# A hybrid three-kind layer stack on one core: the weighted sums of the feed-forward layers run as one block of 24 matmuls instead of three of 8

## The reference, cut to what matters

```python
gating = jax.nn.softmax(x @ W_gate.T, axis=-1)
indicator = jax.nn.one_hot(jnp.argmax(gating, axis=-1), H)
q, k, v = jnp.split(x @ W_qkv.T, 3, axis=-1)
k_shared = jnp.einsum('bth,bthd->btd', indicator, k)
v_shared = jnp.einsum('bth,bthd->btd', gating_top1, v)
att = jnp.einsum('bhqd,bkd->bhqk', q, k_shared) / sqrt(hd)   # 16 heads, hd = 16
att = softmax(where(causal, att, -inf))
y = jnp.einsum('bhqk,bkd->bhqd', att, v_shared)              # the weighted sums
...
x = x + attn_a(layernorm(x)); x = x + ffn(layernorm(x))
x = x + attn_b(layernorm(x)); x = x + ffn(layernorm(x))
```

## Time and profile before

| | before |
|---|---|
| median of 3 runs | 960.64 us (959.54 to 963.05) |
| profiled execution, its own time | 962.72 us |
| span of that execution in the trace | 961.0 us |
| mean granted TensorE clock | 0.972 of full |
| share of the span busy: PE, PEld, DVE, ACT, POOL | 93%, 73%, 74%, 56%, 45% |
| weighted sums of the feed-forward layers, matmul rows | L1748 512, L1751 256 |

### The profile page before, as it was taken

One profiled execution on the slowest core, in us unless ns is written; L12 is line 12 of the kernel. 1 busy time (PEld: TensorE's weight loads), 2 busy tenths in 40 slices (PEclk: granted clock), 3 DMA queues, 4 the chain that ended last, 5 costly groups with the idle time before them and its releaser, 6 DMA issues.

```text
span 961.0 us, 20310 instructions
## 1 busy us (share of the span) xinstructions
PE 891.1 (93%) x6766; PEld 700.0 (73%) x6766; DVE 709.6 (74%) x2331; ACT 534.0 (56%) x1410; POOL 436.4 (45%) x682
## 2 busy tenths in 40 slices
PE   6789989889999999978999999999999997999996
PEld 5677767767767776657878888788878776777763
DVE  6768888888778887664767767685858667888873
ACT  6536554553345455526667676757575762555555
POOL 2458879887756566342202112020202013556655
PEclk9769999999999999989999999999999999999999
DMA  6433333322112555002202020202011021232321
GB/s 197 63 54 56 55 45 55 54 49 43 35 35 58 128 119 139 2 13 45 45 1 45 1 45 2 44 2 45 16 30 41 5 33 32 39 63 47 73 48 35
DMA packets 51287, 46.63 MB, mean 49 GB/s; under 512 B 6624, under 2 KB 48624, under 8 KB 51184
## 3 DMA queue, kind: packets, MB, share of 16 engines
q1 hardware_dynamic: 51184, 45.34, 23.5%
HBM read 11.40 MB, written 2.10 MB: 14 GB/s over the span
## 4 chain that ended last, share of the span: by engine, by line
PE 38%; DVE 10%; issue 4%; ACT 1%; POOL 0%; DMA 0%; POOLq 0%; SPq 0%; ACTq 0%; DVEq 0%
PE bank L285 10%; PE bank L1937 5%; PE bank L1887 5%; PE bank L1945 4%; PE bank L1875 4%; DVE weights L1451 3%; PE bank L1710 3%; PE bank L1722 2%; DVE q_lo L1431 2%; DVE weights L1441 2%; PE bank L1707 2%; PE bank L1748 1%; ACT oT L962 1%; PE bank L1751 1%; DVE arena L1288 1%
## 5 line engine op out<-in xcount | busy, mean ns | idle before, releaser
L1288 DVE TENSOR_REDUCE arena<-bank 128x2 f32<-128x512 f32 (+1 forms) x192 | 130.5, 683 | 43.7 <-PE bank L1710 42.6
L904 ACT ACTIVATE weights<-bank 128x512 f32<-128x512 f32 x144 | 85.7, 596 | 112.9 <-PE bank L1722 111.8
L983 ACT ACTIVATE weights<-weights,neg_max 128x128 f32<-128x128 f32 (+1 forms) x256 | 113.8, 449 | 19.3 <-DVE neg_max L1441 19.3
L1441 DVE CUSTOM_DVE_ANT_0 weights<-bank,arena 128x128 f32<-128x128 f32 (+1 forms) x256 | 80.7, 352 | 56.6 <-PE bank L1937 54.8
L712 POOL TENSOR_SCALAR_AFFINE_SELECT weights<-weights 128x256 f32<-128x256 f32 x144 | 68.2, 475 | 105.0 <-ACT weights L904 104.9
L990 ACT ACTIVATE weights<-bank 128x384 f32<-128x384 f32 x128 | 62.8, 490 | 85.7 <-PE bank L1945 83.5
L1710 PE MATMUL bank<-kf_stack,q_stack 96*128 96x128 f32 (+1 forms) x512 | 109.6, 317 | 0.0
L1937 PE MATMUL bank<-kbT,arena 128*128 128x128 f32 (+1 forms) x512 | 105.1, 328 | 1.1 <-DVE y L420 0.9
L648 POOL TENSOR_SCALAR weights<-weights 128x512 f32<-128x512 f32 x64 | 97.9, 1539 | 12.5 <-ACT weights L807 12.3
L1451 DVE TENSOR_SCALAR weights<-weights,inv_sum 128x128 f32<-128x128 f32 (+1 forms) x256 | 84.3, 371 | 4.5
L285 PE MATMUL bank<-x_hi,wb_hi 128*128 128x256 f32 x256 | 83.5, 326 | 2.8 <-DVE q_lo L1431 2.8
(11 more groups left out here) (232 smaller groups left out, 2443.0 us busy)
## 6 DMA issues: line engine op xcount, KB each, us to landing
q_stack<-q_hi SPq DMA_DIRECT2D x96, 128.0 KB, 3.8
arena<-arena SPq DMA_DIRECT2D x64, 128.0 KB, 2.5
q_stack<-q_lo SPq DMA_DIRECT2D x48, 128.0 KB, 4.0
ka_stack<-k_hi SPq DMA_DIRECT2D x32, 76.5 KB, 3.8
x_all<-x SPq DMA_DIRECT2D x8, 256.0 KB, 5.1
st_wo<-b_wo SPq DMA_DIRECT2D x8, 256.0 KB, 3.1
arena<-b_wqn SPq DMA_DIRECT2D x8, 256.0 KB, 3.2
out<-x_all SPq DMA_DIRECT2D x8, 256.0 KB, 2.1
```

Source lines behind the costliest of these rows:

```text
L904: a.activation(s["pT"][(STEPS * b + k) % N_PT], p2[k % 2][:, :], ACT.Exp).then_inc(s["exp"], 1)
L983: last = a.activation(p, p, ACT.Exp, scale=-1.0, bias=neg_max[:, h % 4, t:t + 1], accum_out=sums[:, h % 4, t:t + 1])
L1288: v.tensor_reduce(into, p1[k % 2][:, :].rearrange("p (h k) -> p h k", h=n), AX.X, ALU.max, negate=True).then_inc(s["maxed"], 1)
L1441: last = v.tensor_tensor_reduce(out=probs[:, h % 4, part], in0=ps_s[h % 2][:, part], in1=mask_b[:, (1 - t) * P:2 * P], scale=1.0, scalar=F ...
```

## The change

`attend_f` loses its argument for the part and runs all three parts back to back. It stands where part 2 stood: octet 1 in step 3, octet 0 in step 9. The matmuls, their operands and the order in which a bank is written are the same; the two waits for the mask become one (all six items instead of four first).

```diff
-                def attend_f(b, o, part):
+                def attend_f(b, o):
...
-                    if part == 0:
-                        pe.wait_ge(*(at(sa, "oT", B - 1, 2) if s is sf[0] and (b, o) == (0, 0) else at(s, "oT", b, o)))
-                        if o == 0:
-                            pe.wait_ge(*at(s, "v_sel", b, 2))
-                    pe.wait_ge(*at(s, "causal", b, 6 * o + (6 if part == 2 else 4)))
+                    pe.wait_ge(*(at(sa, "oT", B - 1, 2) if s is sf[0] and (b, o) == (0, 0) else at(s, "oT", b, o)))
+                    if o == 0:
+                        pe.wait_ge(*at(s, "v_sel", b, 2))
+                    pe.wait_ge(*at(s, "causal", b, 6 * o + 6))
+                    for part in range(2):
+                        for j in range(G):
+                            half = slice(part * T, (part + 1) * T)
+                            mm(ps_o[j * VC:(j + 1) * VC, half], v_sh[b % 3][:, 0, :], items[j][:, half], start=part == 0,
+                               stop=False, skip_group_check=True)
                     for j in range(G):
...
+                        last = mm(ps_o[j * VC:(j + 1) * VC, :].rearrange("p (g q) -> p g q", g=2)[:, :, P:T],
+                                  v_sh[b % 3][:, 1, :],
+                                  items[4 + j // 2].rearrange("p (j g q) -> p j g q", j=2, g=2)[:, j % 2],
+                                  start=False, stop=True, skip_group_check=True)
+                    last.then_inc(s["o_ps"], 1)
...
-                    if k in (1, 3) and there(b - 2):
-                        attend_f(b - 2, 1, (k + 1) // 2)
-                    if k in (5, 7, 9, 11) and there(b - 1):
-                        attend_f(b - 1, k // 11, (k - 5) // 2 % 3)
+                    if k == 3 and there(b - 2):
+                        attend_f(b - 2, 1)
+                    if k == 9 and there(b - 1):
+                        attend_f(b - 1, 0)
```

More of the change, by code:

```diff
@@ L1733, in turn_maxima @@
                     transpose(nm_bank(s, b, o), s["nm"][:, o, :], ident).then_inc(s["nm_ps"], 1)
-                def attend_f(b, o, part):
+                def attend_f(b, o):
                     items = [s["pT"][(STEPS * b + 6 * o + i) % N_PT] for i in range(6)]
-                    if part == 0:
-                        pe.wait_ge(*(at(sa, "oT", B - 1, 2) if s is sf[0] and (b, o) == (0, 0) else at(s, "oT", b, o)))
-                        if o == 0:
-                            pe.wait_ge(*at(s, "v_sel", b, 2))
-                    pe.wait_ge(*at(s, "causal", b, 6 * o + (6 if part == 2 else 4)))
-                    for j in range(G):
[L1745 to L1755, removed]
```

## The result

The changed kernel is slower: 976.7 us (973.6 to 979.7) beside 961.6 (959.5 to 963.1) for the kernel before on the same chip, a ratio of 1.016 with a 95% interval of 1.014 to 1.018. The forecast was 968.8 with a range up to 975.0: the sign was right, and the time lies 1.7 above the range. (The 24 and 8 of the title count rows of the profile; in the program an octet is 12 matmuls and a part 4.) The profiled execution of after took 975.4, its span is 973.7 against 961.0 before.

The account below looks back on a forecast made before the run. A loop of PE (`y` to step 5's scores) and DVE (back to `y`) was taken to bound the kernel. 7.0 + 0.4 + 1.1 - 0.3 = +8.2 on the median 960.64 gave 968.8, 80% range 958.5 to 975.

Parts of the forecast that it names:

- The loop and the cover: Full turn: PE sets time from `y` to step 5's scores, then DVE; parts in steps 5 and 7 cost nothing.
- The turn: Each of eight full turns grows 0.88 us: 0.52 from runs replacing single parts, 0.36 from waiting for `kf_stack`; together +7.0.
- PE's wait for `kf_stack`: Step 0: ACT's L403 and its queue come 0.92 later, and without step 11's part PE waits; +0.36 a turn.
- a part alone costs 0.66: Price of a single part, read in step 11: 0.89 from L1722 on, against 0.23 without a part.
- The clock: Full turns: PE's idle time in steps 7 and 8 grows from 0.5 to about 1.8; a fall costs 1.5 to 2.
- The turn to batch 6: No normalization there, so the part of step 5 counts: 0.88 - 0.66 = +0.22, twice, +0.4.
- I take -0.3 for that end: Second layer's end: -0.8 from the turn to batch 7, at most +0.5 for three parts behind the last masks.
- the -0.8 of the turn to batch 7: No projections there, PE sets the time: two runs replace six single parts, 3.16 - 3.96 = -0.8.
- The first layer's end: Put at +1.1: -0.4 from the turn to batch 7, +0.8 at the lower clock, +0.7 for steps 9 to 3.
- PE bounds everywhere: Rival: PE sets every step, so 0.40 saved per octet is gained 32 times, 12.8, giving 947.8; chance 0.12.
- No change: Rival: `kf_stack` comes early enough and half the shift is absorbed in part of the turns; 960 to 964.2, chance 0.17.
- The rival on the clock: Granted clock falls in two or three of eight turns, 972 to 975, or in all, 981 to 985; chance 0.10.

Follow-up runs that it names:

- e1: The changed kernel with octet 0 back in parts in steps 5, 7 and 9, octet 1 whole in step 3; 961.9 us, ratio 1.000.
- e2: The changed kernel with octet 1 back in parts in steps 11, 1 and 3, octet 0 whole in step 9; 977.4 us, ratio 1.015.
- e5: The kernel before with the parts of steps 5 and 7 left out; 970.5 us beside 961.8, ratio 1.010.
- e6: The changed kernel with ACT's copy of octet 0 (L403) moved behind the copy of kf_stack in step 11; 980.2 us.
- e4: The changed kernel plus two unread PE matmuls in step 7 of seven turns per layer; 972.9 us, ratio 1.011 to before.
- e3: The changed kernel with octet 0's block in step 7 in place of step 9; 961.9 us, ratio 1.000.
- e7: e3 with ACT's copy of octet 0 (L403) in step 8 in place of step 10; 956.9 us, ratio 0.995.
- e8: e7 with octet 1 of the last two batches of each layer left in parts in steps 11, 1 and 3; 955.2 us, ratio 0.994.
- e9: e8 with octet 0 of each layer's last batch also in parts, ACT's copy of it back in step 10; 953.6 us, ratio 0.991.

## Why the prediction was right in its direction and too low

*The loop and the cover: right.* L1733 is still released by `y`, the maximum of step 5 still waits for PE, and e1, e2 and e5 show one by one that the parts of steps 5 and 7 cost nothing where they stood and their full length where they went.

*The turn: +0.88 predicted, +0.72 measured.* The block was priced at 1.58 and measured 1.57; PE's wait for `kf_stack` at 0.36 and measured 0.35. Mis-sized was "a part alone costs 0.66": it was read in step 11 and taken for all four. Before, PE's timeline has in step 9:

```profile
868.49 0.45 PE L1722 MATMUL bank<-q_stack,kf_stack 98*128 98x512 f32 x1
...
869.44 0.28 PE L1707 MATMUL bank<-mask_bf,ident_bf 128*128 128x256 bf16 x1
```

That is 0.95 from L1722 on where step 11 has 0.89, and step 3 has 0.95 too (877.28 to 878.23). The single part of each of these two steps thus cost 0.06 more than it was priced at, together 0.12 of the 0.16 that is left. By octets, e2 has 0.83 where 0.92 was worked out, and e1 -0.10 for -0.04. Eight turns gave 5.8 for 7.0. The maximum of step 5 was to wait longer for PE by 0.4 to 0.9; it waits 0.30 where it waited 0.43, and the longer wait is that of step 10. The prediction's reason for the `kf_stack` wait, ACT's L403 and the queue behind it, was wrong, though its size was right: e6 shows that the exponentials of step 10 hold it.

*The clock: the step that failed.* The prediction saw that PE's idle time in steps 7 and 8 would grow to about 1.8 (measured 1.24 + 0.36 and the 0.23 in which the last matmul still runs), priced a fall at 1.5 to 2 (measured 1.56) and two or three falls at 972 to 975, and then gave that case 0.10 and left the clock out of its sum, because "1.8 is less than 2.30 and is broken up". The one row behind that, 2.30 ahead of a fall, shows that so long a wait was followed by a fall; it says nothing on shorter ones, and the same trace has a wait of 2.05 at 430.40 with no fall behind it. In after the clock fell twice when PE had waited 1.24 and 0.36 (321.53 is one), in e5 six times, and e4 took these two falls away by filling the time. In the profiled execution three falls make 4.9 of the 12.7: these two 3.1, and the one at 287 1.8. That one the prediction has nowhere; PE waits 1.00 and 0.98 there, but e1 and e3 have the same two waits and no fall, and its cause stays open. With the 4.9 the forecast's own sum, 968.8 + 4.9 = 973.7, would have been at the lower edge of the measured runs. Its own sign of being wrong, a granted clock of the full turns below 1, came in two of the eight. By the Trainium skill, "TensorE: Matmul & The Clock Gate", Part 1, being throttled is the default and activity releases it. e4 and e5 agree with that, 1.00 with more work on PE and 0.66 with less. The better question would have been what keeps PE busy in steps 7 and 8, and not how long one wait is.

*The turn to batch 6:* +0.2 predicted, 0.0 measured in the second layer; with 0.72 for the turn in place of 0.88 the same sum gives 0.06. That the part of step 5 counts there is borne out by e5, which lacks it: 18.31 (913.14 to 931.45) where before took 19.08.

*The ends: mis-sized.* "I take -0.3 for that end", of the second layer, measured +1.1. The bound on the block behind the last masks held: from the end of the masks to the end of the program after takes 973.7 - (964.70 + 1.22) = 7.8 and before 961.0 - 953.69 = 7.3, +0.5. PE's timeline in after has the block at the full clock:

```profile
966.07 0.42 PE L1746 MATMUL bank<-weights,v_sh 128*32 128x256 f32 x3 [1.22 <-POOL arena L712]
...
966.93 0.64 PE L1749 MATMUL bank<-arena,v_sh 128*32 128x256 f32 x8
```

What failed is the -0.8 of the turn to batch 7, where PE was to set the time: that turn took 14.99 (935.18 to 950.17) and before 15.07 (923.56 to 938.63), -0.1, and PE now waits 0.19 and 0.20 in it and just behind it for DVE's maxima. From there to the end of the masks after takes another 0.7 more; no run separates why. The first layer's end was put at +1.1 and measured +2.7; the fall of the clock from 438 to 442, which before lacks, is about the difference, as an estimate from the 1.5 to 1.6 that one costs in a turn.

*Luck in the sum.* Without the three falls 7.8 of the 12.7 are left, close to the forecast's +8.2. That is luck: the turns gave 1.2 less, the two ends 3.0 more, and attention b took off 1.5 that stands in no term. And the lower edge of the forecast's own range, 964.5, does not follow from its terms, which add up to 965.3 with +0.52 a turn; nothing hangs on it.

*The rivals.* "PE bounds everywhere" (947.8) falls with e5: 1.3 us less of PE's work in a turn, and the turn did not move. "No change" falls with the result. The rival on the clock was the right one in addition to the forecast, not in its place.

## What to carry to other kernels

Work that stands beside another engine's stretch costs no time there, however dear it looks by itself; merging pieces paid here when the merged piece went to the covered place (e7, step 7), and more when the last batches' pieces stayed spread (e8, e9). Before taking work out of a covered stretch, ask what it did for PE's clock: here time was also lost by leaving the work out altogether (e5), and part of it came back by putting unread work in its place (e4). When a unit moves, move its followers in the other queues with it: ACT's copy, left in step 10, cost e3 0.35 a turn.

## What the runs showed of the hardware that was not expected

The granted clock fell to the lower level after two short waits of PE, 1.24 and 0.36 us with a step's scores between them, and the fall cost 1.5 to 1.6 us each time, in three kernels (after, e5, e6). It did not fall after each such pair: in after it fell behind two of the four in the first layer and behind none of the four in the second, in the profiles of e5 behind six of eight and of e2 behind none, and e2 ran from 970.8 to 978.8 us with a mean clock between 0.972 and 0.962. The length of a single wait does not settle it either: behind 2.18 us ahead of the scores of step 8 of the second layer's first batch the clock fell in e5 (813.46) and not in after (821.07). Why one wait or pair is followed by a fall and the next, of the same length, is not, stays open.
